# Layer seam of a local-attention stack: feed-forward steps inside the attention drain, first chain ahead of the branch

## Chip, cores and metric

The kernel runs on one core of a Trainium2 chip, in one launch. The metric is the device time of an execution in microseconds (us). Its engines are TensorE (PE; PEld is its weight load), VectorE (DVE), ScalarE (ACT), GpSimd (POOL) and SyncE (SP). Each has its own instruction queue, worked in order, and they hand over to one another by semaphores. SP only issues DMAs here.

## The reference

Four parts in sequence, all on 2048 rows of 128 features in float32: a softmax attention, a stack of six layers, a linear attention, and the same stack of six layers again. Nearly all of the time goes to the two stacks. One layer is a local attention and then a feed-forward part:

```python
# tokens shifted by one row in half of the features before both parts
qkv = x @ Wqkv                       # 128 -> 3 * 1024, 16 heads of 64
q = l2norm(q) * qs; k = l2norm(k) * ksc
q, k = rope(q) * 8, rope(k)          # tables cos, sin, scale, and the layer's q and k scales
out = softmax(q k^T, window of 32 + own block of 32) v
x = x + out @ Wo
xn = layernorm(x); a, gate = split(xn @ W1 + b1)
x = x + (a * gelu(gate)) @ W2 + b2   # 341 hidden features
```

## The kernel before

`local_stack` builds one stack; it is called twice, with the tags `f` and `g`. Each engine runs its own program: a prologue, then a hardware loop `Fori(0, DEPTH)` over the six layers, whose body ends in a branch back to its top. The order on each engine is written out by hand. Every semaphore counts a fixed amount per layer, and `upto(s, L, n)` gives the value that step n of layer L stands for.

**Attention.** `tile(L, t, q)` works on tile t (128 rows; NT = 16) in four steps c = 0 to 3. Step n = 4t + c starts one half of the heads of q or k and carries older steps on at fixed lags. On PE: the q or k projection of step n (L1176), transpose of step n-3 (L1181), transpose of the probabilities `pn` of step n-6 (L1190), a V projection at c < 2 (L1198), half of the Wo product of tile t-2 at c >= 2 (L1210), the value product of step n-7 (L1229), the scores of step n-4 (L1244, L1257), and at c = 1 the transpose of the next tile's x (L1165). On ACT: exp (L995), copies (L1005 to L1030), the square (L1016). On DVE: rope products (L1073, L1075), `pn` (L1084), `qh` (L1089), the row maximum (L1095), the sum of squares `ss` (L1102), and at c = 3 the residual `xr` (L1106). On POOL: the power `rn` (L936) and the rope sum `qr` (L941). `rn` of step n needs `ss` of step n, and `qh` of step n needs `rn`.

Because of the lags, tiles 16 and 17 (NT and NT + 1) have no new rows: they are the drain.

**Feed-forward (FF).** `group(L, m, q)` works on groups of 256 rows (NF = 8) in three stages: group m is normalised (DVE L1111 to L1127, with the inverse deviation on POOL, L945 and L947), turned on PE (L1276) and scaled on ACT (L1039, `xnT`); group m-1 goes through three hidden chunks on PE (L1283, L1284), gelu on ACT (L1044) and the gated product `ag` on DVE (L1145); group m-2 through the output matmuls on PE (L1291) and the addition `fy` on DVE (L1135). POOL adds a bias to the residual (L959). In `layer`, group 0 stands between the drain tiles NT and NT + 1, group 1 behind NT + 1, and groups 2 to 10 follow in `groups`. In groups 0 and 1 POOL also folds the next layer's q and k scales into the rope tables (`fold_rope`, L922 and L925; one whole table and two halves each).

**Seam between layers.** SP loads the next projection weights at tile NT (L803), behind them the shifted rows of FF groups 0 and 1 (`load_shifted`), and the FF weights at group NF + 1. At the top of the loop PE transposes tile 0 of the next layer (L1165), ACT copies it (L983), and the steps start. DVE first waits there for the folded rope tables.

Of the kernel before, what the change touches and what calls it, by code (L numbers as in the profile page):

```python
# [626 lines left out]
def local_stack(nc, tag, w, consts, xf, xa):  # L627
# [6 lines left out]
    with ExitStack() as ctx:  # L634
# [29 lines left out]
        ps_h = [[banks[0], banks[7], banks[3]], [banks[4], banks[6], banks[2]]]  # L664
# [92 lines left out]
        def layer(eng, body, group, L, last):  # L757
# [41 lines left out]
        def _(sp):  # L799
# [23 lines left out]
            def tile(L, t, q):  # L823
# [17 lines left out]
                if known and t == NT:  # L841
# [4 lines left out]
                    load_shifted(L, 0, 0)  # L846
                    load_shifted(L, 1, 1)
# [51 lines left out]
            with sp.Fori(0, DEPTH) as L:  # L899
                layer(sp, tile, group, L, NT + 3)  # L900
# [10 lines left out]
        def _(pool):  # L911
# [5 lines left out]
            def fold_rope(n, kind):  # L917

                pool.wait_ge(ld_scales, upto(ld_scales, n, 0, 32))
                whole = qk_scales[:, kind, :].unsqueeze(1).broadcast_to([P, NT, DH])  # L920
                halves = qk_scales[:, kind, :].rearrange("p (a b) -> p a b", a=2)[:, ::-1, :]
                pool.tensor_tensor(rope[:, 2 * kind, :, :], rope0[:, 2 * kind, :, :], whole, ALU.mult).then_inc(pl_rope, 1)  # L922
                for a in range(2):
# [4 lines left out]

            def tile(L, t, q):
                for c in range(4):  # L930
                    n, b = 4 * t + c, c % 2
                    if real(t, c, 0):
# [16 lines left out]
            def group(L, m, q):  # L949
                known = isinstance(m, int)  # L950
                if known and m == 0:
                    inverse_std(L, 0, 0)
                if not known or m + 1 < NF:
                    inverse_std(L, m + 1, 1 - q)
                if not known or 0 <= m - 2 < NF:
# [17 lines left out]
        def _(act):
# [11 lines left out]
            def tile(L, t, q):  # L985
                for c in range(4):
# [26 lines left out]
                    if real(t, c, 0):  # L1013
# [10 lines left out]
                    if real(t, c, 7):  # L1024
# [5 lines left out]
                        act.copy(aT[:, p, 2 * g:2 * g + 2, :], ps_o).then_inc(act_aT, 1)  # L1030

            def group(L, m, q):
                known = isinstance(m, int)
                if known and m == 0:
                    act.wait_ge(ld_wf, upto(ld_wf, L, 0, 13 * 16))
                if not known or m < NF:
                    act.wait_ge(pe_fT, upto(pe_fT, L, m))
                    act.wait_ge(pe_h, upto(pe_h, L, 3 * m - 4))
                    act.activation(xnT[:, q, :], ps_fT[:, 0:FQ], ACT.Identity, bias=ln_b[:], scale=ln_g[:]).then_inc(act_fT, 1)  # L1039
                if not known or 0 <= m - 1 < NF:  # L1040
                    for c, (_, f) in enumerate(HCH):
                        act.wait_ge(pe_h, upto(pe_h, L, 3 * m - 3 + c))
                        act.wait_ge(dv_ag, upto(dv_ag, L, 3 * m - 9 + c))
                        act.activation(gl[0:f, 1 - q, c, :], ps_h[1 - q][c][0:f, 0:FQ], ACT.Gelu,  # L1044
# [676 lines left out]
```

## Time and profile before

| | us |
|---|---|
| median of 3 runs (lowest, highest) | 5260.53 (5259.74, 5274.57) |
| the profiled execution | 5253.03 |
| its span | 5251.2 |
| PE busy | 4463.1 (85%) |
| DVE busy | 3855.7 (73%) |
| ACT busy | 3330.9 (63%) |
| POOL busy | 2830.8 (54%) |

The span runs from the first to the last instruction of the profiled execution; the time around it is 1.8 us. Busy time is counted per engine, and engines overlap. A row of the timeline gives the start, the duration, the engine, the line of the code, the operation with its output and inputs, how many instructions it merges, and in brackets how long the engine had been idle before it and what ended that ("issue": nothing that the profile shows). Matmul ends are modelled, so neighbouring PE rows overlap a little.

### The profile page before, as it was taken

Reading aid. Unit: us, or ns where it says so; the run is one execution under the profiler, and the core shown is the slowest. Engines: PE = TensorE matmul, PEld = TensorE weight load, DVE = VectorE, ACT = ScalarE, POOL = GpSimd, SP = SyncE. Lnnn points to the kernel's source line nnn. Section 1 sums busy time; section 2 is a strip of 40 time slices with the busy share of each in tenths; the row PEclk is TensorE's granted clock in tenths of the full one; section 3 lists DMA queues with packets and bytes.
Section 4 is the critical chain, followed back from the end, with each engine's and each line's share of the span. In section 5 each row is a group of like instructions: output and inputs, shape, how many; then the busy total and the mean of one; then the engine's idle time right before and its main releaser. Section 6 shows DMA issues by size and latency. Waiting matters only on the chain. (4 is left out here: it accounts for less than half of the span.)

```text
span 5251.2 us, 198115 instructions
## 1 busy us (share of the span) xinstructions
PE 4463.1 (85%) x70278; PEld 2798.3 (53%) x70372; DVE 3855.7 (73%) x8097; ACT 3330.9 (63%) x11394; POOL 2830.8 (54%) x2108
## 2 busy tenths in 40 slices
PE   5999999698897988979889656988979889798896
PEld 1333332266565665656656534665656656566565
DVE  7888787486785867858768545867858678587784
ACT  1777777575675766747658413756747668476673
POOL 3000000476675766757667404756757667576673
PEclk6999999898998989989999877989989899898997
DMA  0000000233322323232232302323233223322333
GB/s 13 1 2 1 2 1 1 85 77 83 79 76 79 80 80 78 76 86 73 78 80 76 82 16 89 80 79 76 76 82 80 80 76 80 81 77 78 81 80 91
DMA packets 415346, 340.20 MB, mean 65 GB/s; under 512 B 170606, under 2 KB 312468, under 8 KB 412692
## 3 DMA queue, kind: packets, MB, share of 16 engines
q1 hardware_dynamic: 413972, 332.35, 23.9%
q8 instruction: 350, 5.73, 0.5%
q14 instruction: 256, 2.10, 0.1%
q10 hardware_dynamic: 768, 0.02, 0.0%
HBM read 100.42 MB, written 30.41 MB: 25 GB/s over the span
## 5 line engine op out<-in xcount | busy, mean ns | idle before, releaser
L936 POOL TENSOR_TENSOR f_rn<-f_ss,f_minus_half 128x8 f32<-128x8 f32 x384 | 728.4, 1897 | 397.5 <-DVE f_ss L1102 393.1
L936 POOL TENSOR_TENSOR g_rn<-g_ss,g_minus_half 128x8 f32<-128x8 f32 x384 | 728.7, 1898 | 386.3 <-DVE g_ss L1102 381.9
L427 DVE TENSOR_REDUCE a_maxima<-a_max 128x1 f32<-128x512 f32 x1024 | 651.6, 685 | 149.4 <-PE a_max L541 112.2
L351 ACT ACTIVATE a_pex<-a_scores 128x512 f32<-128x512 f32 x1024 | 531.7, 607 | 162.4 <-PE a_scores L550 161.5
L995 ACT ACTIVATE f_ex<-f_bank,f_nmx 128x64 f32<-128x64 f32 x1536 | 461.2, 314 | 135.8 <-DVE f_nmx L1095 135.3
L995 ACT ACTIVATE g_ex<-g_bank,g_nmx 128x64 f32<-128x64 f32 x1536 | 461.2, 314 | 134.4 <-DVE g_nmx L1095 133.5
L1176 PE MATMUL f_bank<-f_wqkv,f_xT 128*128 128x512 f32 x768 | 442.7, 659 | 92.7 <-DVE f_qh L1089 55.6
L1176 PE MATMUL g_bank<-g_wqkv,g_xT 128*128 128x512 f32 x768 | 442.0, 658 | 91.6 <-DVE g_qh L1089 53.6
L941 POOL TENSOR_TENSOR g_qr<-g_t 128x512 f32<-128x512 f32 x384 | 493.5, 1285 | 8.7 <-DVE g_t L1075 8.7
L941 POOL TENSOR_TENSOR f_qr<-f_t 128x512 f32<-128x512 f32 x384 | 492.2, 1282 | 8.0 <-DVE f_t L1075 8.0
L282 POOL COPY a_v_head<-a_v_all 128x128 f32 (+1 forms) x16 | 4.6, 290 | 697.3 <-PE a_sums L559 697.3
L1089 DVE SCALAR_TENSOR_TENSOR f_qh<-f_rn,f_bank 128x512 f32<-128x512 f32 x384 | 263.4, 686 | 147.6 <-POOL f_rn L936 147.6
L1089 DVE SCALAR_TENSOR_TENSOR g_qh<-g_rn,g_bank 128x512 f32<-128x512 f32 x384 | 263.4, 686 | 145.5 <-POOL g_rn L936 145.0
L541 PE MATMUL a_max<-a_stackT 128*128 128x512 bf16 x963 | 348.1, 398 | 21.1 <-DVE a_maxima L427 12.6
L1229 PEld LDWEIGHTS g_bank<-g_pT,g_vw 64*64 64x64 f32 x12288 | 236.1, 141 | 235.5 <-issue 217.2
L1229 PEld LDWEIGHTS f_bank<-f_pT,f_vw 64*64 64x64 f32 x12288 | 235.2, 140 | 236.3 <-issue 217.4
L550 PE MATMUL a_scores<-a_stackT 128*128 128x512 bf16 x991 | 309.5, 383 | 27.3 <-ACT a_pex L351 20.3
L1229 PE MATMUL f_bank<-f_pT,f_vw 64*64 64x32 f32 x12288 | 268.4, 226 | 69.8 <-ACT f_pT L1012 64.8
L1229 PE MATMUL g_bank<-g_pT,g_vw 64*64 64x32 f32 x12288 | 269.3, 226 | 68.5 <-ACT g_pT L1012 63.6
L995 ACT ACTIVATION_READ_ACCUMULATOR g_ex<-g_bank,g_nmx 128x1 f32 x1536 | 315.1, 205 | 0.0
L995 ACT ACTIVATION_READ_ACCUMULATOR f_ex<-f_bank,f_nmx 128x1 f32 x1536 | 315.1, 205 | 0.0
L1181 PEld LDWEIGHTS g_bank<-g_ident,g_qr 128*128 128x128 f32 x1536 | 196.0, 144 | 206.8 <-issue 133.3
(236 smaller groups left out, 11153.0 us busy)
## 6 DMA issues: line engine op xcount, KB each, us to landing
f_vw<-f_vt SPq DMA_DIRECT2D x576, 128.0 KB
g_vw<-g_vt SPq DMA_DIRECT2D x576, 128.0 KB
f_vw<-f_vt SPq DMA_DIRECT2D x384, 64.0 KB
g_vw<-g_vt SPq DMA_DIRECT2D x384, 64.0 KB
f_wqkv<-in_f_Wqkv_dram SPq DMA_DIRECT2D x7, 1536.0 KB, 8.0
g_wqkv<-in_f_Wqkv_dram SPq DMA_DIRECT2D x7, 1536.0 KB, 8.5
f_xs<-xf SPq DMA_DIRECT2D x196, 32.0 KB, 1.8
g_xs<-xf SPq DMA_DIRECT2D x196, 32.0 KB, 1.8
```

Source lines behind the costliest of these rows:

```text
L282: pool.tensor_copy(v_head[:, p, :, 0:AD], one(v_all, h)).then_inc(pl_vh, 1)
L351: act.activation(pex[:, kt % 2, i % NG, :], ps_s[i % 3][:], ACT.Exp).then_inc(act_ex, 1)
L427: dve.tensor_reduce(maxima[:, m // 4, m % 4:m % 4 + 1], ps_max[m % 3][:], AX.X, ALU.max).then_inc(dv_max, 1)
L541: pe.matmul(ps_max[m % 3][:], stackT[:, slot, 0, P * (m // 4):P * (m // 4) + P], stackT[:, slot, 1, GQ * (m % 4):GQ * (m % 4) + GQ], start ...
L550: pe.matmul(ps_s[i % 3][:], stackT[:, slot, 1, P * kt:P * kt + P], stackT[:, slot, 0, GQ * g:GQ * g + GQ], start=True, stop=True).then_inc ...
L936: pool.tensor_tensor(rn[:, b, :], ss[:, b, :], minus_half[:], ALU.pow).then_inc(pl_rn, 1)
L941: pool.tensor_tensor(qr[:, 1 - b, :], t1[:, 1 - b, :], t2[:, 1 - b, :], ALU.add).then_inc(pl_qr, 1)
L995: last = act.activation(ex[:, 1 - b, u, :], ps_s[:, h, KEYS * jj:KEYS * jj + KEYS], ACT.Exp, bias=nmx[:, 1 - b, u:u + 1], accum_out=sm[:, ...
L1089: dve.scalar_tensor_tensor(out=heads(qh[:, 1 - b, :]), in0=rn[:, 1 - b, :].unsqueeze(2).broadcast_to([P, 8, DH]), scalar=1e12, in1=heads(p ...
L1176: pe.matmul(ps_qk[b][:], xT[:, q, :], wqkv[:, at:at + 512], start=True, stop=True).then_inc(pe_qkv, 1)
L1181: last = pe.transpose(ps_qkT[:, P * j:P * j + P], qr[:, 1 - b, P * j:P * j + P], ident[:])
L1229: last = pe.matmul(ps_o[r, jj, qs], vw[k, p, blk, at:at + DH], pT[k, 1 - b, h, qs], start=True, stop=True, tile_position=(KEYS * jj, DH * h))
```

## The change

Five things, all in `local_stack`:

1. The groups 0 and 1 of the FF are no longer run as whole groups between and behind the drain tiles, except on SP. Their parts (`row_stats`, `normalise`, `turn`, `hidden_in`, `hidden`, `gates`, `gated`; these hold the instructions that `group` had) are called one by one from `during(L, t, c)` behind single steps of tiles NT and NT + 1. POOL does the inverse deviations of groups 0 to 2 behind tile NT.
2. The PSUM banks of the hidden chunks are renumbered.
3. The two first `load_shifted` calls stand one tile earlier on SP.
4. `fold_rope` does one piece per call, in groups 2 to 7.
5. The next layer's first transpose, its copy, the first two projections and the first square, sum and power are issued in groups NF to NF + 2, ahead of the loop's branch; for layer 0 they stand in the prologue.

The diff, cut; the parts named in 1 are left out where they only got a name, and indentation is shortened.

```diff
-ps_h = [[banks[0], banks[7], banks[3]], [banks[4], banks[6], banks[2]]]
+ps_h = [[banks[0], banks[3], banks[7]], [banks[6], banks[4], banks[2]]]
...
-def layer(eng, body, group, L, last):
+def layer(eng, body, group, L, last, inside=False):
...
     for t in range(NT, NT + 3):
         if t < last:
             body(L, t, t % 2)
-        if t < NT + 2:
+        if inside and t < NT + 2:
             group(L, t - NT, t % 2)
...
 # SP
-        load_shifted(L, 0, 0)      # tile NT, behind load_wqkv
-        load_shifted(L, 1, 1)
...
+    if known and t == NT - 1:      # at the end of the tile
+        load_shifted(L, 0, 0)
+        load_shifted(L, 1, 1)
...
 # POOL
+def first_norms(L):
+    pool.wait_ge(dv_ssq, upto(dv_ssq, L, 0)).then_inc(own["pool"], 1)
+    pool.wait_ge(dv_qh, upto(dv_qh, L, -2))
+    pool.tensor_tensor(rn[:, 0, :], ss[:, 0, :], minus_half[:], ALU.pow).then_inc(pl_rn, 1)
...
 def group(L, m, q):
-    if known and m == 0:
-        inverse_std(L, 0, 0)
...
-    if known and m < 2:
-        pool.wait_ge(dv_t2, upto(dv_t2, L, STEPS - 1))
-        fold_rope(L + 1, m)
+    if m - 2 < 6:
+        if m == 2:
+            pool.wait_ge(dv_t2, upto(dv_t2, L, STEPS - 1)).then_inc(own["pool"], 1)
+        fold_rope(L + 1, m - 2)
+    if m == NF + 2:
+        first_norms(L + 1)
 pool.wait_ge(zeroed, 5)
+first_norms(0)
 pool.wait_ge(ld_rope, 16)
-fold_rope(0, 0)
-fold_rope(0, 1)
+for i in range(6):
+    fold_rope(0, i)
+def drained(L, m, q):
+    if m == 2:
+        for k in range(3):
+            inverse_std(L, k, k % 2)
+    group(L, m, q)
...
 # ACT
+def during(L, t, c):
+    if (t, c) == (NT, 3):
+        act.wait_ge(ld_wf, upto(ld_wf, L, 0, 13 * 16))
+        hidden_in(L, 0)
+    if (t, c) == (NT + 1, 1):
+        hidden_in(L, 1)
+    if (t, c) == (NT + 1, 2):
+        gates(L, 0)
+def first_xT(L):                   # in group NF and in the prologue
+    act.wait_ge(pe_xT, upto(pe_xT, L, 0))
+    act.copy(xT[:, 0, :], ps_fT[:, 0:P]).then_inc(act_xT, 1)
+def first_square(L):               # in group NF + 1 and in the prologue
+    act.wait_ge(pe_qkv, upto(pe_qkv, L, 0))
+    act.wait_ge(dv_ssq, upto(dv_ssq, L, -2))
+    act.activation(sq[:, 0, :], ps_qk[0][:], ACT.Square).then_inc(act_sq, 1)
...
 # DVE
+def during(L, t, c):
+    if (t, c) == (NT, 0):
+        row_stats(L, 0, 0)
+    if (t, c) == (NT, 1):
+        normalise(L, 0)
+        row_stats(L, 1, 1)
+    if (t, c) == (NT, 2):
+        normalise(L, 1)
+    if (t, c) == (NT + 1, 0):
+        row_stats(L, 2, 0)
+    if (t, c) == (NT + 1, 1):
+        normalise(L, 2)
+    if (t, c) == (NT + 1, 3):
+        gated(L, 0)
+def first_squares(L):              # in group NF + 1 and in the prologue
+    dve.wait_ge(act_sq, upto(act_sq, L, 0))
+    dve.wait_ge(pl_rn, upto(pl_rn, L, -2))
+    dve.tensor_reduce(ss[:, 0, :], heads(sq[:, 0, :]), AX.X, ALU.add).then_inc(dv_ssq, 1)
...
 # PE
-                    if real(t, c, 0):
+                    if real(t, c, 0) and not (known and n < 2):
...
+def during(L, t, c):
+    if (t, c) == (NT, 2):
+        pe.wait_ge(dv_qh, upto(dv_qh, L, STEPS - 1))
+        pe.wait_ge(ld_wf, upto(ld_wf, L, 0, 13 * 16))
+        turn(L, 0)
+    if (t, c) == (NT, 3):
+        hidden(L, 0, 0)
+        pe.wait_ge(act_qk, upto(act_qk, L, STEPS - 1))
+        hidden(L, 0, 1)
+    if (t, c) == (NT + 1, 0):
+        pe.wait_ge(act_exp, upto(act_exp, L, STEPS - 1))
+        hidden(L, 0, 2)
+    if (t, c) == (NT + 1, 1):
+        turn(L, 1)
+    if (t, c) == (NT + 1, 2):
+        hidden(L, 1, 0)
+def first_xT(L):
+    pe.wait_ge(ld_x[0], upto(ld_x[0], L, 0, 32))
+    pe.wait_ge(act_fT, upto(act_fT, L, -1))
+    pe.transpose(ps_fT[:, 0:P], xs[:, 0, :], ident[:]).then_inc(pe_xT, 1)
+def first_qk(L, n):
+    pe.wait_ge(ld_wqkv, upto(ld_wqkv, L, 0, 16))
+    pe.wait_ge(act_xT, upto(act_xT, L, 0))
+    pe.wait_ge(dv_qh, upto(dv_qh, L, n - 2))
+    at = INNER * KIND[n] + 512 * HALF[n]
+    pe.matmul(ps_qk[n][:], xT[:, 0, :], wqkv[:, at:at + 512], start=True, stop=True).then_inc(pe_qkv, 1)
+def group(L, m, q):
+    if m == NF:
+        first_xT(L + 1)
+    if m < NF:
+        turn(L, m)
+    if m - 1 < NF:
+        for c in range(3):
+            if m == 2 and c == 0:
+                continue
+            if m == 2 and c == 2:
+                pe.wait_ge(dv_y, upto(dv_y, L, NT - 1))
+            hidden(L, m - 1, c)
+    if m == NF + 1:
+        first_qk(L + 1, 0)
+    if m - 2 < NF:
+        outputs(L, m - 2)
+    if m == NF + 1:
+        first_qk(L + 1, 1)
+first_xT(0)
+first_qk(0, 0)
+first_qk(0, 1)
 with pe.Fori(0, DEPTH) as L:
-    transpose_x(L, 0, 0)
-    pe.wait_ge(ld_wqkv, upto(ld_wqkv, L, 0, 16))
```

## Rows read from the trace of the kernel before

**Rows 1.** The page, part 1: busy time of the engines.

```profile
PE 4463.1 (85%) x70278; PEld 2798.3 (53%) x70372; DVE 3855.7 (73%) x8097; ACT 3330.9 (63%) x11394; POOL 2830.8 (54%) x2108
```

**Rows 2.** Timeline of PE, layer 0 of stack f: start, duration, line, operation.

```profile
1243.40 1.06 PE L1210 MATMUL f_bank<-f_wo,f_aT 128*128 128x128 f32 x8
...
1265.32 0.67 PE L1229 MATMUL f_bank<-f_pT,f_vw 64*64 64x32 f32 x32 [0.94 <-ACT f_pT L1012]
...
1265.98 0.45 PE L1257 MATMUL f_bank<-f_kT,f_qT 64*32 64x64 f32 x32
1270.09 0.68 PE L1276 MATMUL f_bank<-f_ident,f_xn 128*128 128x128 f32 x2 [3.66 <-DVE f_xn L1127]
...
1276.88 2.07 PE L1210 MATMUL f_bank<-f_wo,f_aT 128*128 128x128 f32 x8
...
1290.80 0.60 PE L1283 MATMUL f_bank<-f_xnT,f_w 128*128 128x256 f32 x2
...
1293.39 1.50 PE L1291 MATMUL f_bank<-f_w,f_ag 128*128 128x128 f32 x12
1295.14 0.44 PE L1276 MATMUL f_bank<-f_ident,f_xn 128*128 128x128 f32 x2 [0.25 <-DVE f_xn L1127]
...
1322.97 1.57 PE L1291 MATMUL f_bank<-f_w,f_ag 128*128 128x128 f32 x12 [0.70 <-DVE f_fy L1135]
1327.55 0.47 PE L1165 MATMUL f_bank<-f_ident,f_xs 128*128 128x128 f32 x1 [3.01 <-issue]
...
1330.32 1.92 PE L1198 MATMUL f_bank<-f_wqkv,f_xT 128*128 128x512 f32 x2
```

**Rows 3.** Timeline of DVE: first two normalised steps of layer 1.

```profile
1333.80 0.69 DVE L1089 SCALAR_TENSOR_TENSOR f_qh<-f_rn,f_bank 128x512 f32<-128x512 f32 x1 [1.92 <-POOL f_rn L936]
...
1337.41 0.69 DVE L1089 SCALAR_TENSOR_TENSOR f_qh<-f_rn,f_bank 128x512 f32<-128x512 f32 x1 [0.92 <-POOL f_rn L936]
```

**Rows 4.** Windows: length, busy PE, PEld, DVE, ACT, POOL, then clock, DMA share, GB/s.

```profile
1276.00:1283.00 7.00, 6.04 (x80) 5.33 (x80) 0.43 (x2) 0.74 (x2) 0.92 (x1) 0.50 0.01 2
...
1336.00:1350.00 14.00, 10.09 (x103) 4.71 (x102) 10.80 (x20) 7.56 (x26) 12.29 (x9) 1.00 0.34 88
```

**Rows 5.** Timeline of ACT at the same seam.

```profile
1266.12 0.37 ACT L1030 COPY f_aT<-f_bank 128x256 f32<-128x256 f32 x1 [0.94 <-PE f_bank L1229]
...
1284.31 0.56 ACT L1039 ACTIVATE f_xnT<-f_bank,f_ln_b,f_ln_g 128x256 f32<-128x256 f32 x1 [3.90 <-PE f_bank L1276]
...
1323.56 1.28 ACT L983 ACT_TABLE_LOAD   x1 [2.12 <-issue]
...
1332.34 0.58 ACT L1022 COPY f_vt<-f_bank 128x512 f32<-128x512 f32 x1 [1.19 <-PE f_bank L1198]
```

**Rows 6.** Timeline of POOL: prologue of stack f, then the seam.

```profile
993.25 2.48 POOL L925 TENSOR_TENSOR f_rope<-f_rope,f_qk_scales 128x512 f32<-128x512 f32 x2
...
1271.95 2.35 POOL L922 TENSOR_TENSOR f_rope<-f_rope,f_qk_scales 128x1024 f32<-128x1024 f32 x1
...
1297.40 0.73 POOL L959 TENSOR_TENSOR f_fx<-f_fx,f_b 128x256 f32<-128x256 f32 x1
```

**Rows 7.** Timeline of DVE: first `qh` of the stack, two pairs of `xn`.

```profile
998.63 0.69 DVE L1089 SCALAR_TENSOR_TENSOR f_qh<-f_rn,f_bank 128x512 f32<-128x512 f32 x1 [1.91 <-POOL f_rn L936]
...
1288.98 1.49 DVE L1127 TENSOR_SCALAR f_xn<-f_fxs,f_mv,f_rstd 128x128 f32<-128x128 f32 x2
...
1299.12 0.59 DVE L1127 TENSOR_SCALAR f_xn<-f_fxs,f_mv,f_rstd 128x128 f32<-128x128 f32 x2
```

**Rows 8.** Timeline of SP's DMA issues: prologue, end of tile 15, start of tile 16.

```profile
977.46 0.43 SPq L803 DMA_DIRECT2D f_wqkv<-in_f_Wqkv_dram  x1
...
1236.32 0.38 SPq L854 DMA_DIRECT2D f_xr<-xf  x1
...
1245.12 0.55 SPq L833 DMA_DIRECT2D f_vw<-f_vt  x1
```

**Rows 9.** DMA issues of the prologue (970 to 1000): count, KB, us to landing.

```profile
f_wqkv<-in_f_Wqkv_dram SPq DMA_DIRECT2D x1, 1536.0 KB, 12.5
```

More of the change, by code:

```diff
@@ L899, in _ @@
             with sp.Fori(0, DEPTH) as L:
-                layer(sp, tile, group, L, NT + 3)
+                layer(sp, tile, group, L, NT + 3, inside=True)
             for p in range(2):
@@ L915, in _, with fold_rope @@
             pool.memset(kT[:], 0.0).then_inc(zeroed, 1)
-            def fold_rope(n, kind):
+            def fold_rope(n, i):
+                kind, a = i // 3, i % 3 - 1
                 pool.wait_ge(ld_scales, upto(ld_scales, n, 0, 32))
[L920 to L923, printed above, removed]
+                if a < 0:
+                    whole = qk_scales[:, kind, :].unsqueeze(1).broadcast_to([P, NT, DH])
+                    pool.tensor_tensor(rope[:, 2 * kind, :, :], rope0[:, 2 * kind, :, :], whole, ALU.mult).then_inc(pl_rope, 1)
+                else:
+                    halves = qk_scales[:, kind, :].rearrange("p (a b) -> p a b", a=2)[:, ::-1, :]
                     sl = slice(a * 32, a * 32 + 32)
@@ L1030, in tile @@
                         act.copy(aT[:, p, 2 * g:2 * g + 2, :], ps_o).then_inc(act_aT, 1)
-            def group(L, m, q):
[L1033 to L1044, printed above, removed]
-                                       bias=b1[0:f, 3 + c:4 + c]).then_inc(act_gelu, 1)
+                    if known:
+                        during(L, t, c)
@@ L1097, in tile @@
                                           negate=True).then_inc(dv_max, 1)
[L1098 removed]
+                    if real(t, c, 0) and not (known and n == 0):
                         dve.wait_ge(act_sq, upto(act_sq, L, n))
@@ new lines, in gated @@
+            def gated(L, k):
+                dve.wait_ge(ld_wf, upto(ld_wf, L, 0, 13 * 16))
+                for c, (_, f) in enumerate(HCH):
+                    dve.wait_ge(act_gelu, upto(act_gelu, L, 3 * k + c))
+                    dve.wait_ge(pe_out, upto(pe_out, L, k - 2))
+                    dve.scalar_tensor_tensor(out=ag[0:f, k % 2, c, :], in0=ps_h[k % 2][c][0:f, FQ:2 * FQ], scalar=b1[0:f, c:c + 1],
+                                             in1=gl[0:f, k % 2, c, :], op0=ALU.add, op1=ALU.mult).then_inc(dv_ag, 1)
@@ L1261, in tile, with turn @@
                         transpose_x(L, t + 1, 1 - q)
-            def group(L, m, q):
-                known = isinstance(m, int)
-                if known and m == 0:
+                    if known:
+                        during(L, t, c)
+            def turn(L, m):
+                pe.wait_ge(dv_xn, upto(dv_xn, L, m))
+                pe.wait_ge(act_fT, upto(act_fT, L, m - 1))
+                for s in range(FT):
+                    last = pe.transpose(ps_fT[:, P * s:P * s + P], xn[:, m % 2, s, :], ident[:])
+                last.then_inc(pe_fT, 1)
@@ new lines, in hidden, with outputs @@
+            def hidden(L, k, c):
+                f0, f = HCH[c]
+                pe.wait_ge(act_fT, upto(act_fT, L, k))
+                pe.wait_ge(dv_ag, upto(dv_ag, L, 3 * k - 6 + c))
+                pe.matmul(ps_h[k % 2][c][0:f, 0:FQ], w1[:, HID + f0:HID + f0 + f], xnT[:, k % 2, :], start=True, stop=True)
+                pe.matmul(ps_h[k % 2][c][0:f, FQ:2 * FQ], w1[:, f0:f0 + f], xnT[:, k % 2, :], start=True,
+                          stop=True).then_inc(pe_h, 1)
+            def outputs(L, k):
+                pe.wait_ge(dv_ag, upto(dv_ag, L, 3 * k + 2))
+                pe.wait_ge(dv_fy, upto(dv_fy, L, k - 1))
+                for s in range(FT):
+                    for c, (_, f) in enumerate(HCH):
+                        last = pe.matmul(ps_f[:, P * s:P * s + P], ag[0:f, k % 2, c, P * s:P * s + P], w2[0:f, c, :],
+                                         start=(c == 0), stop=(c == 2))
+                last.then_inc(pe_out, 1)
@@ L1286, in group @@
-                if not known or 0 <= m - 2 < NF:
-                    pe.wait_ge(dv_ag, upto(dv_ag, L, 3 * m - 4))
-                    pe.wait_ge(dv_fy, upto(dv_fy, L, m - 3))
-                    for s in range(FT):
-                        for c, (_, f) in enumerate(HCH):
-                            last = pe.matmul(ps_f[:, P * s:P * s + P], ag[0:f, q, c, P * s:P * s + P], w2[0:f, c, :],
-                                             start=(c == 0), stop=(c == 2))
-                    last.then_inc(pe_out, 1)
```

91 lines of the change are left out of this document (47 added, 44 removed).

## The prediction

> **What bounds the kernel now.** I read the page first. It says that TensorE is busy 85% of the span [rows 1], but not where it waits, and the change touches only the seam between attention and feed-forward (FF) and the seam between two layers. These seams come up 12 times (two stacks of six layers). So I read the timelines of one seam engine by engine (layer 0 of the first stack), and checked the same landmarks in three others; they stand at the same distances to within about 1 us. Inside a seam nothing is bound by throughput. It is a chain of single operations that hand over to one another, and three places of it are idle time on TensorE [rows 2]:
> (a) After the last score step (1265.98 + 0.45 = 1266.43) TensorE sits 3.66 us until `xn` of group 0 is there (1270.09). It stands in its queue ahead of the attention's own remaining steps.
> (b) The attention then ends, the FF pipeline fills, and the first regular output matmuls start at 1293.39. From there each group costs about 4.6 us and TensorE waits only 0.25 us per group, for `xn` (1295.14).
> (c) The last output matmuls of the layer end at 1322.97 + 1.57 = 1324.54. The loop's branch costs 3.01 us (1327.55, released by "issue"), and the first chain follows: transpose, projection, square, sum, power. The first `qh` is at 1333.80 and the second at 1337.41 [rows 3].
> The granted clock matters in (a) and (b). It is 0.50 (1.2 GHz) in 1276 to 1283, and a half Wo product takes 2.07 us there (1276.88) against 1.06 us at 2.4 GHz (1243.40) [rows 2, 4].
>
> **Part 1, drain and filling of the FF pipeline (gain).** I take the order in which TensorE gets the work in the new program and start at 1266.43. Up to there only row statistics, two `xn` and one turn (0.44) are added. DVE and PE have more idle time than that in each of these steps, for example 0.94 us on TensorE in front of the last score step's value product (1265.32). From 1266.43 to the output matmuls of group 0, per engine handover [rows 2, 5]:
> - ScalarE ends its copy at 1266.12 + 0.37 = 1266.49 and then does `hidden_in(0)` 0.56: together 0.62.
> - six hidden chunks. One is (1293.39 - 1290.80) / 3 = 0.86, so 5.2.
> - two transposes of `pn` (as the turn, at most 0.44): 0.9. The ScalarE copy behind each, 0.37 and 0.1 for the handover: 0.9.
> - three value products of 0.67: 2.0. Two half Wo products of 1.06: 2.1. Two turns of 0.44: 0.9.
> The sum is 12.6, so the output matmuls start at 1279.0 instead of 1293.39, a gain of 14.4. Gelu's table load and its three activations lie beside the last Wo half, the turn and two chunks. I allow 0.9 for handovers that I do not see and take 13.5.
> The lower bound is the same chain at 1.2 GHz. TensorE's part is 11.1, times 2.07 / 1.06 is 21.7, with ScalarE's 1.5 it is 23.2: start at 1289.6, gain 3.8. I take the fast side because the row nearest to the new mix is 1336 to 1350: TensorE busy 10.09 of 14 us there, granted clock 1.00 [rows 4]. The new drain has it busy some 11 of 12.6, and the long idle (3.66 us) after which the clock fell is gone.
>
> **Part 2, the rope tables move into the FF groups (cost).** Before, GpSimd folds the rope tables in groups 0 and 1 (in the drain). Now it is one piece in each of groups 2 to 7: two whole pieces of 2.35 and four halves of 1.24 (2.48 for two) [rows 6]. In a steady group GpSimd's bias add ends at 1297.40 + 0.73 = 1298.13. A piece then ends at 1300.48 or at 1299.37, and `xn` is due at 1299.12 [rows 6, 7]. Does a GpSimd tensor_tensor hold up `xn`? The row at 1288.98 says so: two `xn` take 1.49 while a piece runs, 0.59 without one. So `xn` comes 1.36 late behind a whole piece and 0.25 late behind a half. TensorE already waits for `xn` in every group (0.25), so this is on the path in full. Five of the six pieces stand ahead of an `xn` (3 to 7): 2 x 1.36 + 3 x 0.25 = 3.5. Bounds: 0 (GpSimd finds another gap) and every piece in full, 2 x 2.35 + 3 x 1.24 = 8.4. I take 3.5.
> The Trainium skill, "SBUF — State Buffer", on the shared port pair, says that this pair is an exclusive lock that whichever of VectorE and GpSimd issues first keeps for its whole instruction. The trace agrees (1.49 against 0.59). By that rule the second of the two `xn` of group 3 could lose the pair again to the piece queued behind the bias add, 2.35 more per layer, 28 us in all; the sum above does not have it.
>
> **Part 3, next layer's first chain ahead of the branch (gain).** The transpose (under 0.3) and the first projection (about 0.95, in a gap of 0.70 in which TensorE waits for `fy`) delay the last outputs by 0.5; the second projection comes behind them, 0.95. Then the branch with its 3.01: the first V product starts at 1324.54 + 0.5 + 0.95 + 3.01 = 1329.0. V (cold, 1.92) ends at 1330.9; its copy 0.58; square of `qk(1)` about 0.6; sum of squares 0.7; power and handover 2.1: second `qh` at 1334.9 instead of 1337.41, a gain of 2.5 [rows 2, 3, 5]. After it the step loop runs as before. Square, sum and power of step 0 lie in the branch time of their engines (ScalarE's is 2.12, then its table load of 1.28, which is over before V is). Bounds: 0.5 (every engine's branch in series) and 4. It applies to 10 seams; a stack's first layer has none.
> The Trainium skill, "Runtime: NRT & Kernel Launch", section Instruction fetch mechanics, says that a taken branch whose target is not in the fetched window stops the engine until a DMA has fetched it. If this fetch starts when the queue reads the branch and not when the last matmul ends, the second projection hides in it and this part is worth 3.5, 10 us more in all. The row shows the 3.01 us but not which of the two.
>
> **Part 4, prologue and exits (cost).** In front of each stack the rope fold now stands behind `first_norms(0)`. The projection weights are issued at 977.46 and land 12.5 later, at 990.0; projection 2.1, square 0.6, sum 0.7, power 1.9: 995.3. The fold of 2 x 2.35 + 2 x 2.48 = 9.6 follows and ends at 1004.9, and the first `qh` waits for it. Before it was at 998.63, with the fold's end at 993.25 + 2.48 = 995.7 [rows 6 to 9]. That is 6 us later, twice: 12. Exits: 0.5 each, 1. Bounds 0 and 16.
>
> **Edits at nothing.** The four shifted loads move on SP from behind the weight load to the end of tile 15. SP has no issue there from 1236.70 to 1245.12 [rows 8], and four take about 2 us. If they slipped they would delay the value windows by so much once. The loads of group 2 now wait for the earlier `xn` of group 0, some 8 us before their first user. The renumbered PSUM banks only change which drain step frees a bank; all are free before the chain of part 1 comes to them. At the layer's start SP still has its FF weight issues to do, and the value windows behind them keep their absolute time; their first user is the value product seven steps on, so a layer that starts 2.5 us sooner is covered, one that starts 10 sooner might not be.
>
> **Sum.** 12 x (13.5 - 3.5) + 10 x 2.5 - 12 - 1 = 132. The profiled execution took 5253.0 (span 5251.2), the median of the runs is 5260.5, 7 above it. I subtract from the median: 5128.
>
> **The rivals.**
> - The port is no matter (13%): GpSimd's pieces fall where DVE works out of PSUM, as the gated products do, or the pieces are short enough. Part 2 is then 0: 42 us better, 5086. For it: the gated products keep their pace beside a piece. Against it: in all steady groups `xn` is due some 1.0 us after the bias add ends, less than any piece.
> - The clock stays down in the drain (18%). Gain of part 1 is then 3.8: 12 x 9.7 = 116 worse, 5244. For it: the old drain stayed at 0.50 from 1276 to 1283 with TensorE busy 6.04 of 7 [rows 4]. In a part of the layers only it gives something between, about 5185.
> - The branch or the queue behind it decides (10%): part 3 gives nothing, since SP, V product or a branch of another engine holds the second step. 25 worse, 5153.
> - The other side, slower (6%): the clock falls in the drain and stays at 1.2 GHz into the FF groups. Before, a thin filling stretch stands between drain and groups and the clock is up when they start (0.86 per chunk at 1290.80); now dense work starts earlier. Part 1 then gives 3.8, part 2 takes 3.5, and each whole group at 1.2 GHz costs 4.1 (TensorE's 4.4 times 0.95). From one such group per layer on it is slower than before: 12 x (0.3 - 4.1) + 25 - 13 = -34, so 5294. Against it: the clock was back 8 us after the stretch at 0.50, through thinner work than will stand there now.
>
> **How the numbers follow.** The forecast has 53%, with its own range of 5100 to 5160 from the bounds of parts 2 and 3. The clock in part of the layers reaches to 5200, and the port rival to 5086 and, with all of part 1, to 5075. So 5072 to 5205 leaves about 2 in 10 outside, nearly all above. What a measurement of this kernel tells from no change is 0.3%, about 16 us. Faster takes the forecast, the port and branch rivals and nearly all of the clock rival, which in full is just at the edge: 0.90. Same 0.04, slower 0.06.
>
> **What would show it.** In the new trace: no TensorE idle over 1 us between the last score step and the first output matmuls, which stand some 12.6 to 14 us apart (part 1). Granted clock 1.00 there; if 0.50, the clock rival. `xn` of 1.5 us and more in two groups per layer, and a TensorE wait for `xn` above 1 us there (part 2). First `qh` within 4 us and second within 10.5 us of the last output matmul's end (part 3). First `qh` of a stack 6 us later from its prologue's start (part 4). The prediction is wrong if the drain's steps get slower by what is put between them, so that the FF work only moves and no idle goes.

## The result and the profile after

| | before | after |
|---|---|---|
| median of 4 runs (lowest, highest), us | 5261.29 (5259.74, 5274.57) | 5184.10 (5172.64, 5198.14) |
| the profiled execution, us | 5253.03 | 5198.14 |
| its span, us | 5251.2 | 5196.3 |
| mean granted clock of TensorE | 0.929 | 0.934 |

The ratio is 0.9849, with a 95% interval of 0.9818 to 0.9880: 77 us faster by the medians, 55 us between the two profiled executions. The one profiled after is the slowest of its four runs. Busy times hardly move; the first part of the page after answers to [rows 1]:

```profile
PE 4459.6 (86%) x70382; PEld 2776.0 (53%) x70382; DVE 3876.7 (75%) x8099; ACT 3326.2 (64%) x11398; POOL 2834.6 (55%) x2110
```

VectorE gained 21 us of busy time with only two instructions more: it is being held up somewhere. Where this happens shows at a few landmarks of each of the 12 layers: last `qh`, first output matmuls, last `fy`, second and eighth `qh` of the next layer. Means over the layers in us (the seam over the ten that have one), for all kernels of this study:

| kernel | last `qh` to first outputs | to last `fy` | the 8 pairs of `xn` | last `fy` to second `qh` | second to eighth `qh` |
|---|---|---|---|---|---|
| before | 40.48 | 31.01 | 5.15 | 12.47 | 23.01 |
| after | 25.31 | 38.07 | 8.71 | 9.87 | 26.09 |
| e1 piece behind `xn` | 25.68 | 32.19 | 5.15 | 9.68 | 25.99 |
| e2 pieces nearly empty | 25.66 | 32.45 | 5.41 | 9.50 | 26.31 |
| e3 whole pieces in four | 25.78 | 35.06 | 6.77 | 9.84 | 26.30 |
| e4 matmuls into the wait | 24.80 | 35.74 | 8.71 | 9.34 | 26.11 |
| e5 no early chain | 25.51 | 37.89 | 8.64 | 12.10 | 23.73 |
| e6 early table load | 26.05 | 38.19 | 8.71 | 8.71 | 26.68 |
| e7 fold first in prologue | 25.02 | 38.00 | 8.71 | 9.61 | 25.76 |
| e8 later FF weights | 25.48 | 37.67 | 8.71 | 9.92 | 25.10 |
| e9 = e1 + e6 + e7 + e8 | 25.79 | 32.19 | 5.15 | 8.34 | 23.94 |
| e10 = e1 + e5 + e8 | 25.50 | 32.07 | 5.16 | 12.42 | 22.88 |
| e11 = e1 + e6 + e7 | 25.49 | 32.19 | 5.15 | 8.28 | 26.89 |

After against before in the profiled executions: the drain gives 15.2 x 12 = 182, the FF stretch takes 7.1 x 12 = 85, the seam gives 2.6 x 10 = 26, the steps behind it take 3.1 x 12 = 37, the rest of the attention 1.4 x 12 = 17, the two prologues 6.5 x 2 = 13, and the parts outside the stacks 2. The balance is 55 faster (the terms are rounded), as measured. A prologue is taken from the issue of the projection weights to the first `qh`: 21.2 and 21.7 us before, 27.6 and 28.3 after. The absolute time of a `qh` would not do, since what runs ahead of stack f ends up to 5 us sooner or later in one kernel than in another.

**The drain.** TensorE in layer 0 of stack f after, from the last score step on; it answers to [rows 2]:

```profile
1277.57 0.46 PE L1335 MATMUL f_bank<-f_kT,f_qT 64*32 64x64 f32 x32
1278.68 0.69 PE L1354 MATMUL f_bank<-f_xnT,f_w 128*128 128x256 f32 x2 [0.66 <-ACT f_xnT L1056]
...
1281.44 0.67 PE L1307 MATMUL f_bank<-f_pT,f_vw 64*64 64x32 f32 x32 [0.55 <-ACT f_pT L1031]
...
1283.91 0.67 PE L1307 MATMUL f_bank<-f_pT,f_vw 64*64 64x32 f32 x32 [0.55 <-ACT f_pT L1031]
...
1284.78 1.06 PE L1288 MATMUL f_bank<-f_wo,f_aT 128*128 128x128 f32 x8
...
1290.18 1.50 PE L1363 MATMUL f_bank<-f_w,f_ag 128*128 128x128 f32 x12
1295.12 0.69 PE L1347 MATMUL f_bank<-f_ident,f_xn 128*128 128x128 f32 x2 [3.45 <-DVE f_xn L1175]
1295.60 1.06 PE L1354 MATMUL f_bank<-f_xnT,f_w 128*128 128x256 f32 x2
1296.45 1.06 PE L1355 MATMUL f_bank<-f_xnT,f_w 128*128 128x256 f32 x2
```

From the end of the last score step (1278.03) to the first outputs are 12.15 us. No wait in between is over 0.66, and the half Wo product takes 1.06. Right behind them is what the forecast did not have: 3.45 us idle on TensorE, and then half chunks every 0.85 us instead of every 0.43. The windows (columns as in [rows 4]) give the granted clock: 0.50 in a part of the drain ahead of the last score step, 1.00 from that step to the first outputs, and 0.66 behind them:

```profile
1265.00:1270.00 5.00, 3.79 (x106) 2.94 (x106) 4.01 (x10) 2.70 (x12) 2.46 (x4) 0.50 0.62 196
...
1276.00:1292.00 16.00, 13.13 (x226) 10.93 (x224) 6.48 (x23) 9.33 (x29) 1.88 (x5) 1.00 0.16 40
1292.00:1302.00 10.00, 6.88 (x24) 5.53 (x25) 5.53 (x12) 1.98 (x4) 5.83 (x6) 0.66 0.37 105
1302.00:1326.00 24.00, 21.61 (x133) 18.58 (x132) 14.54 (x40) 9.60 (x20) 13.01 (x16) 1.00 0.26 72
...
1332.00:1342.00 10.00, 7.29 (x9) 2.24 (x10) 3.77 (x6) 3.81 (x6) 3.08 (x2) 0.50 0.27 53
```

All twelve layers agree. The chain takes 12.15 to 12.17 us at 1.00 in each. Each has the wait of 3.45 us, and in the 10 us from the start of that `xn` pair the clock is 0.66 in eight layers and 0.83 in four. From the last `qh` to the end of the last score step are 13.5 us before and 13.2 after on the mean, so the FF work put between these steps does not make them longer.

**The held pair.** The pair of `xn` that TensorE waits for, on VectorE:

```profile
1292.03 3.04 DVE L1175 TENSOR_SCALAR f_xn<-f_fxs,f_mv,f_rstd 128x128 f32<-128x128 f32 x2
```

The same two on their own, in the answer for that tile (durations in ns, lowest, median, highest):

```profile
L1175 DVE TENSOR_SCALAR f_xn<-f_fxs,f_mv,f_rstd x2: 742/1558/2374, 1292.0 to 1292.7; 128x128 f32<-128x128 f32 x2
```

GpSimd beside it, the bias add and the rope piece of group 2:

```profile
1291.97 0.72 POOL L966 TENSOR_TENSOR f_fx<-f_fx,f_b 128x256 f32<-128x256 f32 x1
1292.65 2.34 POOL L925 TENSOR_TENSOR f_rope<-f_rope,f_qk_scales 128x1024 f32<-128x1024 f32 x1
```

The first `xn` (742 ns) ends within 0.1 us of the bias add, the second (2374 ns) within 0.1 us of the piece.

**The seam.** TensorE at the loop's branch after, then ScalarE, then `qh` on VectorE, answering to [rows 2, 3, 5]:

```profile
1327.07 1.57 PE L1363 MATMUL f_bank<-f_w,f_ag 128*128 128x128 f32 x12
1328.48 1.02 PE L1395 MATMUL f_bank<-f_wqkv,f_xT 128*128 128x512 f32 x2
1331.82 1.97 PE L1276 MATMUL f_bank<-f_wqkv,f_xT 128*128 128x512 f32 x2 [2.32 <-issue]
1335.82 2.08 PE L1276 MATMUL f_bank<-f_wqkv,f_xT 128*128 128x512 f32 x2 [2.04 <-ACT f_vt L1041]
...
1338.85 3.58 PE L1254 MATMUL f_bank<-f_wqkv,f_xT 128*128 128x512 f32 x4
```

```profile
1333.89 1.28 ACT L1041 ACT_TABLE_LOAD   x1 [6.03 <-PE f_bank L1276]
1335.19 0.58 ACT L1041 COPY f_vt<-f_bank 128x512 f32<-128x512 f32 x1
1335.67 0.60 ACT L1035 ACTIVATE f_sq<-f_bank 128x512 f32<-128x512 f32 x1
```

```profile
1332.18 0.69 DVE L1138 SCALAR_TENSOR_TENSOR f_qh<-f_rn,f_bank 128x512 f32<-128x512 f32 x1 [2.71 <-issue]
...
1339.12 0.69 DVE L1138 SCALAR_TENSOR_TENSOR f_qh<-f_rn,f_bank 128x512 f32<-128x512 f32 x1 [0.92 <-POOL f_rn L946]
...
1344.31 0.69 DVE L1138 SCALAR_TENSOR_TENSOR f_qh<-f_rn,f_bank 128x512 f32<-128x512 f32 x1 [0.93 <-POOL f_rn L946]
```

Before, the second `qh` came 3.61 us behind the first [rows 3]. Now it comes 6.94 behind and the third 5.19 behind that, with the clock at 0.50 from 1332 to 1342.

### The profile page after: what moved, and what is told of

It is laid out like the page before. It is cut to its first block and busy times, and to the rows that moved or that the text cites. A ratio compares the mean times of both kernels' runs of the same rounds, so it can differ in the third digit from the quotient of the medians.

```text
span 5196.3 us, 198441 instructions
## 1 busy us (share of the span) xinstructions
PE 4459.6 (86%) x70382; PEld 2776.0 (53%) x70382; DVE 3876.7 (75%) x8099; ACT 3326.2 (64%) x11398; POOL 2834.6 (55%) x2110
## 5 line engine op out<-in xcount | busy, mean ns | idle before, releaser
L1254 PE MATMUL f_bank<-f_wqkv,f_xT 128*128 128x512 f32 x744 | 431.9, 665 | 71.9 <-DVE f_qh L1138 51.8
L541 PE MATMUL a_max<-a_stackT 128*128 128x512 bf16 x1024 | 367.4, 396 | 14.3 <-DVE a_maxima L427 7.4
L550 PE MATMUL a_scores<-a_stackT 128*128 128x512 bf16 x1024 | 319.6, 383 | 24.8 <-ACT a_pex L351 23.9
```

Of the source, the lines that this page charges most:

```text
L541: pe.matmul(ps_max[m % 3][:], stackT[:, slot, 0, P * (m // 4):P * (m // 4) + P], stackT[:, slot, 1, GQ * (m % 4):GQ * (m % 4) + GQ], start ...
L550: pe.matmul(ps_s[i % 3][:], stackT[:, slot, 1, P * kt:P * kt + P], stackT[:, slot, 0, GQ * g:GQ * g + GQ], start=True, stop=True).then_inc ...
L1254: pe.matmul(ps_qk[b][:], xT[:, q, :], wqkv[:, at:at + 512], start=True, stop=True).then_inc(pe_qkv, 1)
```

## The experiments

Each is an edit of the changed kernel, timed against the kernel before on the same chip. They ran in three batches (e1 to e4, e5 to e8, e9 to e11), so they are compared with each other as ratios to before.

### e1, e2, e3, e4: what does a rope piece cost the FF groups?

e1: each piece waits until the `xn` of the group that is normalised at that time is done.

```diff
+                    if m + 1 < NF:
+                        pool.wait_ge(dv_xn, upto(dv_xn, L, m + 1))
                     fold_rope(L + 1, m - 2)
```

> The rope pieces stay in groups 2 to 6 but wait on GpSimd until xn of the next group is done. Port theory (a piece holds the port that xn needs, and the 3.45 us that TensorE then sits drop its clock for group 3): the pair of xn in group 3 takes 0.6 to 0.9 instead of 3.04 us, no group runs at 1.2 GHz, first output matmuls to last fy falls from 38.1 to about 31.5 us, and the kernel is 12 x 6.5 = 78 us faster than the changed one, about 5105. Rival (the groups slow down because the pipeline now starts with less lead, whatever GpSimd does): that stretch stays above 36 us and the time within 20 us of 5184.

Measured: 5116.29 us, ratio 0.9726 (0.9709 to 0.9742). The FF stretch falls from 38.07 to 32.19. The piece, the `xn` pairs of groups 3 and 4, the turn of group 3 and the clock window of e1 there (GpSimd, VectorE, TensorE, windows):

```profile
1290.84 2.36 POOL L925 TENSOR_TENSOR f_rope<-f_rope,f_qk_scales 128x1024 f32<-128x1024 f32 x1 [0.52 <-DVE f_xn L1177]
```

```profile
1289.66 1.00 DVE L1177 TENSOR_SCALAR f_xn<-f_fxs,f_mv,f_rstd 128x128 f32<-128x128 f32 x2
...
1294.69 0.59 DVE L1177 TENSOR_SCALAR f_xn<-f_fxs,f_mv,f_rstd 128x128 f32<-128x128 f32 x2
```

```profile
1290.72 0.44 PE L1349 MATMUL f_bank<-f_ident,f_xn 128*128 128x128 f32 x2 [1.40 <-DVE f_xn L1177]
```

```profile
1293.00:1303.00 10.00, 9.50 (x58) 8.07 (x57) 6.28 (x22) 4.36 (x9) 7.58 (x12) 1.00 0.39 106
```

The piece is as long as before and is on GpSimd all the same. Standing behind `xn` it costs nothing, and the clock stays at 1.00, in all twelve layers. The pair of group 3 still takes 1.00 instead of 0.59, since the bias add stands ahead of the piece and runs beside it.

e2: inside the layers the folds work on one tile of the rope table instead of all 16. It leaves out the scaling of the other 15, so it bounds the price of the pieces and is no kernel to use. The edit, cut:

```diff
-whole = qk_scales[:, kind, :].unsqueeze(1).broadcast_to([P, NT, DH])
+whole = qk_scales[:, kind, :].unsqueeze(1).broadcast_to([P, 1, DH])
```

> Leaves out the rope fold inside the layers but for one table row per piece (the layers' scales are all ones, so the tables do not change). Bound for what the pieces cost. Port theory: as with the pieces behind xn, the stretch is about 31 us, about 5100; the difference between the two runs is what the pieces cost even in the good place, under 10 us. Rival: still above 36 us.

Measured: 5120.34, ratio 0.9727 (0.9710 to 0.9743). With nearly all of the work left out it is no faster than e1: what a piece costs here is its place. (The expectation says that the tables do not change. That is not shown here, and the reading doesn't need it.)

e3: a whole piece is cut into four instructions of four tiles each.

```diff
-pool.tensor_tensor(rope[:, 2 * kind, :, :], ...)
+for k in range(4):
+    last = pool.tensor_tensor(rope[:, 2 * kind, r, :], ...)   # r: tiles 4k to 4k + 3
```

> The two whole pieces are cut into four instructions each, same place and same elements. If the port is held for one instruction and given back between instructions, the pair of xn of group 3 takes about 1.2 to 1.9 instead of 3.04 us, TensorE idles under 2.5 us, its clock stays up and about 4 to 5 us per layer come back, 50 us in all, about 5135. If it is traffic that slows VectorE as long as GpSimd works, the pair still takes about 3 us and nothing comes back, about 5184.

Measured: 5154.38, ratio 0.9796 (0.9779 to 0.9812). `xn` 6.77, FF stretch 35.06: half comes back. The pair of group 3 and the four instructions beside it:

```profile
1288.37 1.42 DVE L1178 TENSOR_SCALAR f_xn<-f_fxs,f_mv,f_rstd 128x128 f32<-128x128 f32 x2
```

```profile
1288.99 2.77 POOL L927 TENSOR_TENSOR f_rope<-f_rope,f_qk_scales 128x256 f32<-128x256 f32 x4
```

The pair is over at 1289.79, while GpSimd works until 1291.76. So the length of one instruction decides how long `xn` is held, and not how long GpSimd is busy. TensorE still waits 1.84 us for it, and in nine of twelve layers the clock falls behind that wait (0.83 in the 10 us from the start of the pair). In the other three it stays at 1.00.

e4: seven matmuls whose result nobody reads stand in TensorE's queue ahead of the turn of group 3, where it waits.

```diff
+if m == 3:
+    for k in range(7):
+        pe.matmul(banks[0][:, 0:FQ], w1[:, 0:P], w1[:, 0:FQ], start=True, stop=True)
 if m < NF:
     turn(L, m)
```

> Seven extra matmuls (128x256, about 3.0 us) in TensorE's idle time ahead of the turn of group 3; their result is overwritten. The pieces stay. Clock theory: TensorE stays at 2.4 GHz, the hidden chunks of group 3 take 0.86 instead of 1.7, and the layer gets 3.5 us shorter although work was added, 42 us in all, about 5142; the pair of xn still takes 3.04. Rival (the slow group 3 has another cause than TensorE's idle time): no gain, or some us slower, 5184 to 5195.

Measured: 5152.02, ratio 0.9792 (0.9775 to 0.9808). The window of e4 at the same times as above:

```profile
1292.00:1302.00 10.00, 9.50 (x57) 8.03 (x57) 6.33 (x21) 4.33 (x10) 6.42 (x10) 1.00 0.33 88
```

`xn` is held exactly as long as in the changed kernel (8.71), but the clock does not fall in any layer, and the FF stretch is 2.3 us shorter (3.5 were expected). So the 5.9 us that e1 brings back are 2.3 of half clock after the wait, and the rest, 3.6, is what `xn` is held less (8.71 - 5.15).

### e5, e6, e7, e8: the seam and the prologue

The ratios of these four are 0.9818 to 0.9834, and the interval of each overlaps that of the changed kernel, 0.9818 to 0.9880. So no time in this part tells an edit from no edit. What is read are the distances in the profiled executions.

e5: part 5 of the change undone; transpose, both projections, square, sum and power stand behind the branch again.

> The changed kernel without its fifth part: the first chain of a layer stands behind the branch again and the prologue is the old one; the drain and the rope pieces stay as changed. Theory (the part gains nothing: what it gains up to the second qh, 2.6 us, is given back by step 7 because V products, their copies and the next projection stand in one chain on a cold TensorE, and the prologue loses 8 us per stack): last fy to eighth qh of the next layer within 1 us of the changed kernel's 36.0, and the whole kernel 10 to 25 us faster than the changed one, about 5165. Rival (the part is worth its 2.5 us per seam as forecast): about 5184 + 25 - 12 or more, 5195 to 5200.

Measured: ratio 0.9830 (0.9807 to 0.9853). From the last `fy` to the eighth `qh` are 12.10 + 23.73 = 35.8 us, in the changed kernel 9.87 + 26.09 = 36.0. As it stands the early chain is worth nothing: what it gives up to the second `qh` is gone by the eighth, and each prologue is 6.3 us shorter without the part.

e6: an activation of one column that nobody reads opens ScalarE's loop body, ahead of its first wait, and takes the table load with it.

```diff
 with act.Fori(0, DEPTH) as L:
+    act.activation(early[:], ident[:, 0:1], ACT.Exp)
     act.wait_ge(dv_kzero, upto(dv_kzero, L, -1))
```

> One exp of a 128x1 tile without a wait is put first behind ScalarE's branch. Theory: the table load of 1.28 us stands behind the wait for the first V product in the changed kernel, so it is on the path; now it runs during that wait, the second qh comes 1.3 us sooner after the last fy (9.87 to about 8.6), 10 seams, 13 us in all, about 5171. Rival (the load ends in time anyway, or something else holds the second step): no change of that distance.

Measured: ratio 0.9818 (0.9802 to 0.9835). ScalarE of e6 at the seam; its first V copy follows the V product without the load:

```profile
1327.56 1.28 ACT L1104 ACT_TABLE_LOAD   x1 [2.40 <-issue]
1328.85 0.20 ACT L1104 ACTIVATE f_early<-f_ident 128x1 f32<-128x1 f32 x1
1330.68 0.59 ACT L1042 COPY f_vt<-f_bank 128x512 f32<-128x512 f32 x1 [1.62 <-PE f_bank L1278]
```

The second `qh` comes 1.2 us sooner (8.71 against 9.87), which is the load. Half of it is gone again by the eighth: the steps behind take 0.6 more.

e7: the six folds stand ahead of `first_norms(0)` in GpSimd's prologue.

> first_norms(0) stands behind the six rope pieces of the prologue. Theory: the fold starts when the rope table lands, first qh of stack f at about 998 instead of 1006.3 and the same 8 us in stack g, 15 us in all, about 5169. Rival (the weight load holds both): first qh stays within 2 us of 1006.

Measured: ratio 0.9820 (0.9802 to 0.9838). The changed kernel's prologue on GpSimd, with its power ahead of the folds:

```profile
995.01 1.64 POOL L936 TENSOR_TENSOR f_rn<-f_ss,f_minus_half 128x8 f32<-128x8 f32 x1 [17.90 <-DVE f_ss L1206]
...
1003.65 2.46 POOL L929 TENSOR_TENSOR f_rope<-f_rope,f_qk_scales 128x512 f32<-128x512 f32 x2
```

GpSimd sits 17.90 us idle ahead of it. With the folds in that gap the first `qh` comes 20.5 and 20.1 us behind the issue of the projection weights in the two stacks, after 27.6 and 28.3 in the changed kernel and 21.2 and 21.7 before. So 7.7 us per stack come back, 1.2 more than the change had cost.

e8: SP issues the FF weights of a layer at the end of its tile 2, instead of in the group ahead of the branch.

```diff
-if known and m == NF + 1:          # with its two waits
-    load_wf((L + 1) % DEPTH)
...
+if known and t == 2:
+    sp.wait_ge(dv_fy, upto(dv_fy, L - 1, NF - 1))
+    load_wf(L)
```

> The 13 issues of the FF weights move on SP from the layer's end to the end of tile 2. Theory: they hold up the value-window loads of tile 0, for which ScalarE waits in front of its copy of tile 1 (5.65 us in layer 10 of the changed kernel); without them the second to eighth qh take about 23.5 us instead of 26.1 on the mean and the layers with 28 to 31 go away, 20 to 30 us in all, about 5158. Rival (the cold TensorE alone makes these steps slow): 26 us as before, within 8 us of 5184.

Measured: ratio 0.9834 (0.9817 to 0.9850). What it acts on is in three layers only. ScalarE, TensorE and SP's issues of the changed kernel in the second last layer of stack g:

```profile
4530.34 0.58 ACT L1041 COPY g_vt<-g_bank 128x512 f32<-128x512 f32 x1 [5.65 <-DMA g_vw<-g_vt]
```

```profile
4530.97 2.08 PE L1276 MATMUL g_bank<-g_wqkv,g_xT 128*128 128x512 f32 x2 [3.98 <-ACT g_vt L1041]
```

```profile
4507.31 0.37 SPq L813 DMA_DIRECT2D g_w<-in_f_W_dram  x1
...
4516.01 0.38 SPq L821 DMA_DIRECT2D g_b<-in_f_b_dram  x1
...
4521.08 0.60 SPq L833 DMA_DIRECT2D g_vw<-g_vt  x1
```

The weight issues keep SP busy from 4507.31 to 4516.4, the value windows go out from 4521.08 on, and a V copy, and with it TensorE, waits for one. In the three such layers the second to eighth `qh` take 28.2, 30.3 and 29.2 us; in e8 they take 25.2 to 25.4. The other nine stay as they were, so the mean is 25.1 and not the 23.5 expected. The edit does one thing more: SP no longer issues 13 loads for nobody behind the last layer of a stack, and from the last `fy` of stack g to the kernel's end are 20.2 us instead of 27.2.

### e9, e10, e11: the edits together

e9 holds the edits of e1, e6, e7 and e8. e10 holds those of e1, e8 and e5. e11 is e9 without that of e8.

> Four edits on the changed kernel together: each rope piece waits behind the xn of its group, ScalarE's table load stands at the top of its loop body, the fold stands ahead of first_norms(0) in the prologue, and SP issues the FF weights behind tile 2 of the layer. If the four costs are separate, the gains add: ratios to the kernel before were 0.9726 for the first alone (changed kernel 0.9849), 0.982, 0.982 and 0.9834 for the other three, so 0.9726 - 0.003 - 0.003 - 0.0015 = 0.965, with first qh of a stack at about 994, xn near 5.2 us per layer, and first to eighth step of a layer below 26 in all layers. Rival: the seam is one chain on a starved TensorE, so what the early table load gives up to the second qh comes back by the eighth step, and only the fold counts: 0.970 to 0.972.

> Rope pieces behind xn and FF weights behind tile 2, but part 5 (the first chain ahead of the branch) undone. If part 5 is worth nothing, as its removal alone let it seem (0.983 against 0.9849), this gives the same as e9 or up to 0.003 less or more: 0.965 to 0.970. Rival: the seam's gain of 2.6 us per layer was only eaten by the table load and the fold; with these mended e9 is ahead of this by 10 x 2.6 = 26 us, 0.005.

> As e9 but with the FF weights where the changed kernel has them. If the late value windows of three layers in each stack are on the path, e9 is faster than this by 3 x 3 to 6 x 3 us, 9 to 18 (0.002 to 0.003). Rival: they are made up for later in the layer: no difference.

| | median (lowest, highest), 5 runs | ratio to before (95%) |
|---|---|---|
| e9 | 5059.24 (5054.34, 5061.60) | 0.9610 (0.9596, 0.9624) |
| e10 | 5078.61 (5069.95, 5092.23) | 0.9650 (0.9631, 0.9669) |
| e11 | 5100.48 (5098.21, 5108.21) | 0.9690 (0.9676, 0.9705) |

e9 beats both kernels: 205 us under before. That is more than the 0.965 of adding up the four gains, so the costs are not quite separate: later FF weights take 1.0 us off the steps from second to eighth `qh` in e8, and 2.95 beside the other edits (e9 against e11). e9 against e10 says that the early chain is worth 19 us after all, nearer the rival's 26 than nothing, once the load, the fold and the weight issues are out of its way: last `fy` to eighth `qh` takes 32.3 us with it and 35.3 without. e9 against e11 says that later FF weights are worth 41 us, over twice the 9 to 18 expected. By the profiled executions 35 of it are in these steps, because a layer that starts sooner meets the late windows more often: 26.9 us from second to eighth `qh` against 23.9, and over 26 in seven of twelve layers. Another 7 are the loads left out at the kernel's end. TensorE and the windows of e9 at the seam:

```profile
1313.92 1.02 PE L1398 MATMUL f_bank<-f_wqkv,f_xT 128*128 128x512 f32 x2
1317.50 1.12 PE L1279 MATMUL f_bank<-f_wqkv,f_xT 128*128 128x512 f32 x2 [2.56 <-issue]
1319.37 1.91 PE L1279 MATMUL f_bank<-f_wqkv,f_xT 128*128 128x512 f32 x2 [0.75 <-ACT f_vt L1043]
```

```profile
1316.00:1326.00 10.00, 7.08 (x11) 2.46 (x12) 4.40 (x7) 3.68 (x7) 3.29 (x3) 0.68 0.23 56
1326.00:1336.00 10.00, 7.42 (x94) 3.77 (x93) 7.72 (x16) 5.84 (x18) 9.15 (x6) 0.98 0.28 73
```

The wait between the two V products is 0.75 instead of 2.04, and the clock is back in the second stretch. It still falls in the first.

## Why the prediction was partly right

The direction and the main mechanism were right, and 5184 is within the range. But 132 us were forecast and 77 came (55 in the profiled executions). Part 1 gave 20 more. The FF stretch took 38 more than forecast, the steps behind the second `qh` 37, the rest of the attention 17, the seam itself 4, and the prologues and the parts outside the stacks 2. The forecast's own range ended at 5160. Only the rival of a clock that stays down in the drain took it to 5205, and that rival did not come, so that 5184 lies within it is in part luck.

**Part 1, right, a little low.** The chain took 12.15 us (forecast 12.6) at a clock of 1.00, and the drain is 15.2 us shorter per layer (forecast 13.5), since the 0.9 set aside for unseen handovers was not needed. That is 20 us more than forecast.

**Part 2 is the first step that failed: a term is missing, and its weight stood in the wrong place.** The sum of the `xn` came out right, 8.71 against 5.15 in e1, 3.6 per layer (forecast 3.5). But it was forecast in even parts (1.36 per whole piece), and instead 2.45 fall on group 3, where the bias add held the first `xn` and the piece the second. That is the rule of the Trainium skill, "SBUF — State Buffer", on the shared port pair, which the prediction named and left out of its sum. The trace agrees with it: 742 and 2374 ns for two instructions that take 0.59 us together. Its extra 28 us did not show as a sum: group 3 took 1.1 more per layer than forecast, and the other groups together 1.0 less. Its real harm was to put one wait of 3.45 us in one place: the clock fell, and the group behind it ran at half clock. That is 2.3 us per layer by e4, 28 in all. "TensorE waits for `xn`, so it is on the path in full" priced the wait and not what TensorE does after it. The remaining 1.2 of the FF stretch is still there in e1 (32.19 against 31.01). The early projection is 0.12 of it (e10: 32.07), and nearly all of the rest is one wait: TensorE stands 1.40 for the `xn` of group 3 in e1, against 0.25 in a steady group before. Forecast for the stretch were 3.5 in each of 12 layers and 0.5 at 10 seams, 47 us. Measured: 85.

**Part 3, nearly right up to the second `qh`; behind it stands the second step that failed.** Forecast were 1334.9 - 1325.04 = 9.9 us from the last outputs' end to the second `qh`, measured 1339.12 - 1328.64 = 10.48. The gain of 2.5 had the outputs' delay of 0.5 in it already, which here is counted in the FF stretch, so from the last `fy` on 3.0 were forecast and 2.6 came. Two errors nearly cancel in it. V starts 3.18 us behind the last outputs (1331.82 - 1328.64), where the sum had 0.95 + 3.01 = 3.96. The projection lies almost whole beside the branch. That is the case which the prediction left open behind the branch rule of the Trainium skill, "Runtime: NRT & Kernel Launch"; the rule doesn't say when the fetch starts, and no row here shows a fetch. And the table load, which "is over before V is", stands behind V. That was read from the kernel before, where the load ran at 1323.56 [rows 5], 4 us before TensorE began the transpose (1327.55) that the copy behind it waits for. Part 5 made the V copy the first activation of the layer, and there ScalarE came to the load only when V was over. That is 1.28 us on the path. Then, "after it the step loop runs as before" was false: the steps to the eighth `qh` take 3.1 us more. e5 shows that this is tied to part 5 (23.73 without it). With the value windows out of the way it falls by 1.0 (e8), and with the other edits beside that one 0.9 is left (e9). How much of this is the table load's place and how much the clock, no run tells.

**Edits at nothing.** That SP's windows "keep their absolute time" was right: in stack f they go out 10.2 to 11.2 us behind the last `fy` before and 10.3 to 10.8 after. That "a layer that starts 2.5 us sooner is covered" was not: the seam was priced as if it were, and the windows were on the path in three of twelve layers. The shifted loads and the banks cost nothing that shows.

**Part 4, right.** 6.5 us per stack, forecast as 6. e7 shows that all of it, and 1.2 us more, could be had by the order.

**The rivals.** The port did matter; only another place of the piece (e1) brings that rival's price of 0 for part 2. The clock did fall in the drain, but ahead of the last score step, as it had before the change (0.50 in 1255 to 1260 then, in 1265 to 1270 now), and it was back for the chain of part 1 in all twelve layers. The prediction, which put the fall down to the long idle of 3.66 us, did not look at this one. Then it fell behind the drain, for one group per layer; the slower side needed such a group together with a cold chain and did not come. The branch rival ("part 3 gives nothing, since SP, V product or a branch of another engine holds the second step") is what part 3 came to in sum, though a few steps later than it said.

What stays open: why the rest of the attention took 1.4 us more per layer. That stretch lies between 227.5 and 229.7 in all these kernels, with single layers of the changed kernel from 224 to 235, and no edit here acts on it. Also open is what the low clock behind the branch costs. On the mean of the ten seams it is 0.95 in the second 10 us from the last `fy` on before, 0.70 after, 0.66 in e8 and 0.82 in e9. No edit acts on it alone.

## What to carry to other kernels

Place a side engine's long operation right behind the instruction that it would hold up, not at the first gap of its own queue: one wait line was worth 65 us here, and leaving nearly all of the work out gave no more. Price a new wait of TensorE together with the work behind it at half clock. And when a chain is moved up, look at what stands next in each queue behind it (a table load behind a wait, a block of DMA issues), because until those move too the gain can be given back within a few steps.

## What the runs showed of the hardware

- One GpSimd operation after another can hold up successive VectorE operations one by one: 742 and 2374 ns for two that take 0.59 us together when alone. Cut into four, GpSimd's long one holds the pair 1.42 us instead of 3.04, though it works longer (2.77 against 2.34).
- The granted clock at one place behind four waits of TensorE, twelve layers each: with 3.45 us it fell in all (0.66 or 0.83 in the 10 us from the start of the `xn` pair), with 1.84 in nine (e3, 0.83), with 1.40 in none (e1), and with matmuls that nobody reads put into the wait in none (e4). Where it fell to 0.66, the six matmul pairs behind the turn start every 0.85 us instead of every 0.43.
- The table load of 1.28 us stands with the first activation behind the branch, but not always on the same side of its wait. Before, it ran at 1323.56, ahead of the end of the wait for TensorE's transpose. After, it ran only when V was there (1333.89), and the copy behind it has two semaphore waits where the earlier one had one. Whether that is the reason was not tried. An activation without a wait at the top of the loop (e6) takes the load ahead of the wait for V.
- A matmul pair of 1.02 us issued ahead of a loop's branch lengthens the way from the work ahead of it to the first matmul behind it by 0.1 to 0.3 us on the mean of ten seams (3.04 after and 3.16 in e9, against 2.90 before; single seams differ by up to 0.7 within one kernel).
